# Four fused transformer layers on one core: the rotary exchange of the first attention moves from VectorE to ScalarE and GpSimd, its clamp of the maxima to VectorE, and preparations are spread

## The reference

```
Q, K, V = proj(wq), proj(wk), proj(wv)          # of layernorm(x), 16 heads of 16
Q = Q * cos + _rotate_half(Q) * sin             # _rotate_half: [-x2, x1]
K = K * cos + _rotate_half(K) * sin
scores = einsum(Q, K) / sqrt(hd)                # only keys < 25 and keys >= 128
probs  = softmax(scores)
# V[t > 128] += V[128] * (bern_u < p) / 128     # p from the last row of probs
x = x + nan_to_num(einsum(probs, V) @ wo.T)
```

## Time and profile before

| | us |
|---|---|
| median of 3 runs (range) | 981.79 (980.92 to 987.29) |
| the profiled execution | 981.94 |
| its span, first to last instruction | 980.2 |
| PE busy / DVE busy / ACT busy / POOL busy | 896.0 / 739.2 / 547.5 / 374.5 |

### The profile page before, as it was taken

How to read it: one execution, slowest core, us unless ns; L and a number is a source line. 1 busy time by engine, 2 the same in 40 slices (tenths; PEclk the granted TensorE clock), 3 DMA queues, 4 the chain that set the end, 5 groups by cost and what they waited for, 6 DMA issues and landing times.

```text
span 980.2 us, 20069 instructions
## 1 busy us (share of the span) xinstructions
PE 896.0 (91%) x6646; PEld 710.4 (72%) x6646; DVE 739.2 (75%) x2389; ACT 547.5 (56%) x1426; POOL 374.5 (38%) x560
## 2 busy tenths in 40 slices
PE   6787898988999999977999999999999997999996
PEld 5576676767776777655878787888888776776763
DVE  6677888888888898564867676676858677889973
ACT  5456456554554555435575666767575762555554
POOL 4367578875634444244202021211202000344444
PEclk9878889998999999979999999999999999999999
DMA  6431333222111655102102020202020111222321
GB/s 203 69 53 38 44 54 53 47 39 41 34 35 41 130 119 124 40 13 44 27 19 44 2 44 1 45 1 45 1 44 20 26 26 25 52 59 50 70 48 34
DMA packets 51286, 46.61 MB, mean 48 GB/s; under 512 B 6624, under 2 KB 48624, under 8 KB 51184
## 3 DMA queue, kind: packets, MB, share of 16 engines
q1 hardware_dynamic: 51184, 45.34, 22.8%
HBM read 11.40 MB, written 2.10 MB: 14 GB/s over the span
## 4 chain that ended last, share of the span: by engine, by line
PE 35%; DVE 12%; issue 4%; ACT 1%; POOL 0%; DMA 0%; POOLq 0%; SPq 0%; ACTq 0%; DVEq 0%
PE bank L283 9%; PE bank L1886 5%; PE bank L1838 5%; PE bank L1894 4%; PE bank L1826 3%; DVE weights L1410 3%; DVE q_lo L1390 2%; PE bank L1661 2%; PE bank L1673 2%; DVE weights L1400 2%; PE bank L1658 1%; DVE arena L1239 1%; PE bank L1699 1%; ACT oT L935 1%; PE bank L1702 1%
## 5 line engine op out<-in xcount | busy, mean ns | idle before, releaser
L877 ACT ACTIVATE weights<-bank 128x512 f32<-128x512 f32 x144 | 85.8, 596 | 121.2 <-PE bank L1673 119.9
L1239 DVE TENSOR_REDUCE arena<-bank 128x2 f32<-128x512 f32 (+1 forms) x192 | 129.1, 679 | 28.8 <-PE bank L1661 28.6
L956 ACT ACTIVATE weights<-weights,neg_max 128x128 f32<-128x128 f32 (+1 forms) x256 | 113.8, 449 | 19.5 <-DVE neg_max L1400 19.5
L1400 DVE CUSTOM_DVE_ANT_0 weights<-bank,arena 128x128 f32<-128x128 f32 (+1 forms) x256 | 80.8, 354 | 56.6 <-PE bank L1886 54.8
L697 POOL TENSOR_SCALAR_AFFINE_SELECT weights<-weights 128x256 f32<-128x256 f32 x144 | 67.4, 469 | 129.4 <-ACT weights L877 129.2
L963 ACT ACTIVATE weights<-bank 128x384 f32<-128x384 f32 x128 | 62.7, 490 | 85.6 <-PE bank L1894 83.3
L1661 PE MATMUL bank<-kf_stack,q_stack 96*128 96x128 f32 (+1 forms) x512 | 110.4, 319 | 0.0
L1886 PE MATMUL bank<-kbT,arena 128*128 128x128 f32 (+1 forms) x512 | 105.1, 328 | 1.0 <-DVE y L418 0.9
L648 POOL TENSOR_SCALAR weights<-weights 128x512 f32<-128x512 f32 x64 | 96.9, 1522 | 14.6 <-ACT weights L790 14.6
L1410 DVE TENSOR_SCALAR weights<-weights,inv_sum 128x128 f32<-128x128 f32 (+1 forms) x256 | 83.8, 370 | 4.5
L283 PE MATMUL bank<-x_hi,wb_hi 128*128 128x256 f32 x256 | 83.6, 327 | 2.8 <-DVE q_lo L1390 2.8
(11 more groups left out here) (227 smaller groups left out, 2422.3 us busy)
## 6 DMA issues: line engine op xcount, KB each, us to landing
q_stack<-q_hi SPq DMA_DIRECT2D x96, 128.0 KB, 3.8
arena<-arena SPq DMA_DIRECT2D x64, 128.0 KB, 2.6
q_stack<-q_lo SPq DMA_DIRECT2D x48, 128.0 KB, 4.0
ka_stack<-k_hi SPq DMA_DIRECT2D x32, 76.5 KB, 3.1
x_all<-x SPq DMA_DIRECT2D x8, 256.0 KB, 5.1
st_wo<-b_wo SPq DMA_DIRECT2D x8, 256.0 KB, 3.6
arena<-b_wqn SPq DMA_DIRECT2D x8, 256.0 KB, 3.7
out<-x_all SPq DMA_DIRECT2D x8, 256.0 KB, 2.1
```

What stands on the lines that cost most here:

```text
L956: last = a.activation(p, p, ACT.Exp, scale=-1.0, bias=neg_max[:, h % 4, t:t + 1], accum_out=sums[:, h % 4, t:t + 1])
L1239: v.tensor_reduce(into, p1[k % 2][:, :].rearrange("p (h k) -> p h k", h=n), AX.X, ALU.max, negate=True).then_inc(s["maxed"], 1)
L1400: last = v.tensor_tensor_reduce(out=probs[:, h % 4, part], in0=ps_s[h % 2][:, part], in1=mask_b[:, (1 - t) * P:2 * P], scale=1.0, scalar=F ...
```

## The change

**Exchange.** `exchange` on DVE is gone. ACT copies each half of the bank into the other half's partitions (`swap`, two instructions of 64 partitions, keys in step 2 ahead of its other work, queries in step 5 ahead of its other work), and POOL multiplies the copy in place by the sines (one instruction of 128 partitions) in `rotated`, ahead of the sum. The table of sines has its signs turned for that. PE's waits for the exchanged half (`values_a`, `last_token`, `spread_row`) become waits for the copies.

**Clamp.** It moves from POOL to DVE, right behind the maxima of heads 7 and 15.

**Places.** On POOL the inverse root goes from step 6 to step 7, behind `rotated` of the queries, and the residual of b-3 from step 7 to 9. On DVE the normalisation goes from step 8 to 9 and `dve_shift_lo` from 10 to 11; SP's rows of maxima from 11 to 12. The first keys' projection of sequence 1 goes from PE's step (-1, 15) to (0, 0).

**Preparations.** The split of the feed-forward weights goes from (2, 4) to (2, 8) and (2, 11), the fills from (3, 4) to (3, 5), (3, 10), (3, 11) and (4, 10). In `weights_b` statistics, inverse root and normalisation of attention B's first sequence go from k = 9, 10, 11 to k = 0, 1, 2, and PE's transpose of it waits for four parts of `wb_lo`, the projection (h = 3) for all six.

```diff
             def rotated(b, n):
...
+                n_t, table = (T, C_SIN) if n == "q" else (KA_PAD, C_SINK)
+                pool.wait_ge(*at(sa, n + "_swap", b, 1))
+                g.tensor_tensor(r2, r2, cst[:, table:table + n_t].unsqueeze(1).to_broadcast([P, NC, n_t]), ALU.mult)\
+                    .then_inc(sa[n + "_rot2"], 1)
                 pool.wait_ge(*at(sa, n + "_rot1", b, 1))
...
-                if k == 0 and there(b - 1):
-                    clamp(b - 1, 1)
-                if k == 8 and there(b):
-                    clamp(b, 0)
...
+            def swap(b, n):
+                n_t, r, bank = (T, rot2, ps_b) if n == "q" else (KA_PAD, krot2, ps_a)
+                act.wait_ge(*at(sa, n + "_rot1", b, 1))
+                for into, of in ((slice(0, P // 2), slice(P // 2, P)), (slice(P // 2, P), slice(0, P // 2))):
+                    last = a.activation(r[into], halves(bank)[of, :, 0:n_t], ACT.Copy)
+                last.then_inc(sa[n + "_swap"], 1)
...
+            def clamp(b, o):
+                dve.wait_ge(*at(sa, "maxed", b, (o + 1) * OCT))
+                v.tensor_scalar(nm[:, o, :], nm[:, o, :], CLAMP, -CLAMP, ALU.min, ALU.max).then_inc(sa["clamped"], 1)
...
-            def exchange(b, n):
...
-                if (b, k) == (2, 4):
+                if (b, k) == (2, 8):
                     dve.wait_ge(s_fsplit, 2)
                     split_turned(f_lo, st_f, f_hi, 0, s_fsplit)
+                if (b, k) == (2, 11):
...
             def weights_b(k):
+                if k == 0:
+                    dve_stats(sm, 0)
+                if k == 2:
+                    dve_normalize(sm, 0)
...
                     last.then_inc(b_lo, 1)
-                    dve_stats(sm, 0)
...
                 if h == 1:
                     if b == 0:
-                        pe.wait_ge(b_lo, 6)
+                        pe.wait_ge(b_lo, 4)
                         pe.wait_ge(b_mvo, 4)
```

More of the change, by code:

```diff
@@ L520, in step_a @@
                     sp_stack(b + 1, "q", 0)
-                if k == 11 and there(b):
+                if k == 12 and there(b):
                     sp_put_shift(sa, b, 0)
@@ L662, in step_a @@
                     low(b + 1, "k")
[L663 to L666 removed]
                 if k == 7 and there(b + 1):
                     rotated(b + 1, "q")
+                if k == 7 and there(b + 2):
+                    pool_rstd(sa, b + 2)
                 if k == 9 and there(b + 1):
@@ L671, in step_a @@
                     last_query(b + 1)
+                if k == 9 and there(b - 3):
+                    residual(sa, b - 3, guard_t, at(sa, "guarded", b - 3, 5))
                 if k == 13 and b > -2 and there(b + 2):
@@ L823, in step_a @@
                     a.activation(a_hi[:, :, A_V:A_COLS], st_a[:, :, A_V:A_COLS], ACT.Copy).then_inc(s_split, 1)
+                if k == 2 and there(b + 1):
+                    swap(b + 1, "k")
+                if k == 5 and there(b + 1):
+                    swap(b + 1, "q")
                 if (b, k) == (2, 3):
@@ L1184, in step_a @@
                     rotate(b + 1, "k")
-                if k == 2 and there(b + 1):
-                    exchange(b + 1, "k")
                 if k == 1 and there(b - 2):
@@ L1198, in step_a @@
                     rotate(b + 1, "q")
-                if k == 4 and there(b + 1):
-                    exchange(b + 1, "q")
                 if k == 5 and there(b + 2):
@@ L1224, in step_a @@
                     maximum_a(b, k)
+                    if k % OCT == OCT - 1:
+                        clamp(b, k // OCT)
             def ffn(s):
```

55 lines of the change are left out of this document (22 added, 33 removed).

## The result

| | before | after |
|---|---|---|
| median of 4 runs (range), us | 981.36 (980.75 to 987.29) | 970.50 (970.31 to 971.53) |
| ratio of the times, 95% interval | | 0.988 (0.985 to 0.991) |
| span of the profiled execution, us | 980.2 | 968.6 |
| mean granted TensorE clock | 0.960 | 0.970 |

The kernel is 1.2% faster, some 11 us. The forecast was 964, or 18 less; the range of 948 to 980 holds the result. So the sign was right, and more than a third of the gain is missing. First, where it is: the busy times on the page of the changed kernel.

What follows compares the result with a forecast made beforehand. Rounds were taken as bound by DVE's dense stretch and the line POOL sum, ACT, PE. Terms -10.2, -1.0, +1.1, -4.0 and -4.0 sum to -18.1, from 981.94 to 964 us; forecast's own range 956 to 971, whole range 948 to 980.

Steps and rivals of the forecast that it cites:

- DVE's dense stretch: DVE's work from step 0 to 9 of a round, one of two things said to set its length.
- the line POOL sum, ACT high part, exponentials, PE: Chain through POOL, ACT and PE's steps 10 and 11, the other thing said to set a round.
- Part 1: Exchange leaves DVE: per round DVE's work falls 23.1 to some 21.2 us, ACT gets 2.1, POOL goes 21.8 to 23.8.
- Part 2: New round step by step: queries' sum ends at 14.4 instead of 16.5, round 1.7 us shorter, 25.9 us.
- six rounds (b = 1 to 6) make 10.2: In attention A, rounds b = 1 to 6 gain 1.7 us each, 10.2 us together.
- model round: Middle round of attention A without preparations, 27.6 us, from which the gain of a round was worked out.
- Part 3: Start: rotation of sequence 0, on the path to the first scores, takes 1.1 us longer.
- Parts 4 and 5: Feed-forward split and fills spread, 4.0 us off; first sequence normalised earlier ahead of attention B, 4.0 us off.
- Rival B: Ring comes loose: clock stays up, rounds fall from 27.6 to 24.4 us, time 950 us; chance 0.16.
- A: POOL gives back DVE's win: PE stands in steps 10 and 11, low clock follows, rounds keep length, 975 us; chance 0.22.
- C: POOL and DVE hinder each other: long DVE instructions, decisive if DVE waits over 4 us at normalisation; 998 us; chance 0.08.

Runs made afterwards that it cites:

- the last kernel: Changed kernel with the exchange back on DVE and the clamp back on POOL in its old steps; 965.38 us, ratio 0.983 to the kernel before.
- the four kernels: Changed kernel (970.50 us), it with the start set back (966.63), with the exchange back on DVE (964.68), and with both (965.21).
- the single edits: Kernel before with only the feed-forward split and fills spread (977.35 us, ratio 0.991), and with only attention B's first preparation moved (977.93 us, ratio 0.995).

## Why the prediction was right and where it failed

**What bounds the kernel** was read rightly, the weights were not. I named two things that set a round, DVE's dense stretch and the line POOL sum, ACT high part, exponentials, PE. The second decides in the rounds b = 3 to 5, in all kernels but the last: the next round starts 11 us after the sum, 12.1 to 12.6 with the low clock in the tail. The first acts in two ways. With the exchange on DVE the sum of rounds 4 and 5 comes 0.8 and 1.0 us later, behind a stand of PE for L357 and the low clock after it. And where the sum comes early something else sets the round, by the traces DVE: round 6 takes 27.0 us with a sum that ends at 13.2 or at 14.3, and a round of the last kernel 27.0 at full clock with DVE busy for 25.5. I had taken the two as bounds of like weight in every round. PE's wait for L357 in step 3 comes ahead of its stand in step 10, so what is won at the first has still to pass the second.

**Part 1** had the durations right. Copies of half the partitions take as long as whole ones, 0.44 and 0.60 us each (0.9 and 1.2 forecast, 0.88 and 1.20 measured). POOL's work came out at 22.4 to 22.8 instead of 23.8, since its keys' sum took 0.87 instead of 1.24, and the keys' product 0.86. In the round before, DVE's bound lay beside that sum (171.47 beside 171.37); now it lies beside a guard. The clamps take 0.37 on average (0.17 and 0.37 in the 25.0 us round), not 0.2. None of it mattered.

**Part 2** had the sum's end right (14.0 to 14.1, forecast 14.4), named the cause rightly (inverse root and residual behind the sum), and was right in size for b = 2 to 5, 10.4 measured for 10.8 with the preparations. The run with the inverse root first shows the cause: that one move is worth 8 to 10 us over the whole. What failed is the step "six rounds (b = 1 to 6) make 10.2". The gain of 2.1 us rested on a residual to move, on POOL's wait of 2.7 us for the keys' high part to hide the keys' product, and on the sum being what the round waits for. In round b = 1 there is no residual yet and that wait is 0.6 us, so both products lie in front of the sum: it ends at 16.4 instead of 15.8, the tail grows by 1.2, and the round by 1.7. In b = 6 the inverse root is one of the next layer, which the change did not move, and the sum ends at 14.6 where it ended at 14.3. But there an earlier sum alone changes nothing (27.0 us with it at 13.2), so its move could not give the 1.7 us. These two rounds are 5.0 us of what is missing. I had multiplied a model round without asking of each round whether its conditions held.

The credit was given wrongly, too. I gave the exchange 2.4 us of relief on DVE, and a delay of the sum which POOL's idle time would hide in part. In rounds 4 and 5 about 1 us of relief reaches the sum, in 2 and 3 none. Over the whole the exchange costs 6 to 8 us, most of it at the start and in round 1, and the order of POOL's queue has to earn that back.

**Part 3** was mis-sized: +1.1 forecast, +4.95 measured at the first gate. By the four kernels with and without each edit, the exchange's way costs 2.2 to 2.4 of it, twice the forecast, which had counted the queries' rotation alone. The other 2.5 to 2.7 us are a step missing from the working: I had moved inverse root and normalisation by a step in the rounds and not looked at what stands in that step at the start. The trace of before has the split of the weights (L1033) at 8.68, right behind the normalisation at 6.87, itself waiting for ACT; the listing of the new order has the two the other way round.

**Parts 4 and 5** were right by the traces: 4.0 and 4.0 forecast, 3.8 and 4.1 off the profiled spans of the single edits. By the ratios they are 9 (6 to 12) and 5 (3 to 7), so part 4 may be larger than forecast.

**Some of it was luck.** Round 0 and the stretch of b = 7 gave 3.1 us more than forecast, for which no part of the working gives a reason. Without them the time would have been about 973.6, outside the forecast's own 956 to 971, though still in the range of 948 to 980. Rival B's sum is not right either: with the 8 us of parts 4 and 5 it comes to 954, the 950 takes 12 for them.

**The rivals.** A was right about the mechanism, PE standing in step 10 and the low clock behind it, and wrong in that the rounds do not keep their length: the low clock takes 1.0 to 1.5 us of a tail, not the whole gain. B did not happen; among the middle rounds of the changed kernel the 25.0 us at full clock is the shortest. C did not either: the wait at the normalisation is 2.15 us, under its point of 4. Its long DVE instructions are there, the bound took 1.51 us beside POOL, against a least of 0.40, and both normalising ones 1.02. They fall into time in which DVE would have waited.

## What to carry to other kernels

When several engines wait for each other in a ring, look for an instruction from which the rest of the round has a fixed length, and price every edit by what it puts ahead of it or takes away from ahead of it in its engine's queue. Then ask where that stops: once the instruction comes early enough, another engine sets the round, here most likely DVE. Go through the rounds one by one, first and last above all: a model round holds only where all the moved instructions exist, the waits that hide the new ones are there, and the same engine is waited for. A change of several parts should be taken apart even when it wins, because here the part in its title cost 6 to 8 us and the small moves beside it paid.

## What the hardware showed

- **The low clock follows the stand, but not every time.** In the 4 us up to the end of its stand ahead of step 10 PE was busy for 1.88 us in one round and 1.89 in the next, at a clock of 1.00 in both; the 4 us behind it had 0.68 in the first case and 1.00 in the second. What makes the difference is not seen. The tail of the round took 12.5 and 11.0 us. Ahead of attention B, where PE's stand for the normalised sequence went, 3.1 us were won at the first projection and 3.9 behind the stretch that had run at 0.50 and 0.64. And small moves make rounds jump between 25.0 and 26.7 us. No run changed the clock by itself, so its price is read from rounds of different clock, not shown by an experiment.
- **Half the partitions save nothing on ScalarE.** 64x512 from PSUM took 0.593 us on average, 128x512 0.597. An exchange of halves therefore cost as much as two full copies. VectorE has the same price for the old form (two times 0.689 for 64 partitions); one rotation product of 128 partitions took 0.673.
- **VectorE and GpSimd stretch each other.** The bound (128x512 from SBUF to SBUF) took 1.51 us beside POOL's product in rounds 1, 4 and 5, and the product 1.28 to 1.29. With the exchange back on DVE no product stands on POOL, and the same instruction, now beside the inverse root, took 0.41 in each of the rounds 1 to 5. The other way round, POOL's keys' sum took 1.24 us with a bound of 0.40 beside it, and 0.87 in the new kernel without one. The Trainium skill, "Advanced Engine Details and Errata", section "VectorE Performance Modes", says that the second VectorE port is shared with GpSimd, and that GpSimd instructions and VectorE's two-port ones block each other. The trace agrees: one engine takes longer by 1.1 us beside an instruction of 1.29, and by 0.37 beside one of 0.40. The edit moved other instructions as well, so the port itself is not isolated as the cause.
